# A softplus of which one VectorE operation becomes a sum of two products in PSUM, in a fused Mamba and feed-forward kernel

## What is computed

```python
x, z = split(hidden @ in_proj_w.T)              # 512 channels each
u = silu(causal_conv4(x) + conv_b)
dt_lo, B, C = split(u @ x_proj_w.T)             # 64, 16, 16
delta = softplus(dt_lo @ dt_proj_w.T + dt_proj_b)
h[t] = exp(delta[t] * A) * h[t-1] + delta[t] * u[t] * B[t]   # 512 x 16 states
y = (sum_n h * C + u * D) * silu(z)
x1 = layernorm(hidden + y @ out_proj_w.T)
f = gelu(gelu((silu(x1 @ w1) * (x1 @ w2)) @ h1) @ h2) @ w3   # with a scale per column
out = layernorm(x1 + f)
```

## Time and profile before

| | us |
|---|---|
| median of 3 runs (3010.54 to 3012.91) | 3012.06 |
| the profiled execution | 3011.42 |
| its span, first to last instruction | 3009.6 |
| mean granted clock of TensorE | 0.953 |

### The profile page before, as it was taken

The page is one execution under the profiler, slowest core; times in us unless marked ns, Lnnn a source line. Parts: engine busy times, 40 slices in busy tenths (PEclk is TensorE's granted clock), DMA queues, the critical chain, the costliest instruction groups (busy, mean ns, idle before and its releaser), DMA issues. The chain is left out here.

```text
span 3009.6 us, 40984 instructions
## 1 busy us (share of the span) xinstructions
PE 2720.0 (90%) x11540; PEld 1619.3 (54%) x11540; DVE 2297.7 (76%) x2650; ACT 2033.7 (68%) x3600; POOL 1704.2 (57%) x839
## 2 busy tenths in 40 slices
PE   5798998998998998998998976999999999999997
PEld 2243443343443443443443432778888888888886
DVE  6999999999999999999999999144445444444452
ACT  3878877878878877877878877465544555555452
POOL 4899999999899989999999998100000000000000
PEclk8899999998999999999999987999999999999999
DMA  8565565565566565565565566632222222222210
GB/s 265 122 188 158 144 190 158 144 193 164 134 193 165 136 192 159 139 196 158 139 192 165 143 186 224 205 101 77 92 70 70 84 91 77 70 79 88 70 42 15
DMA packets 239646, 412.05 MB, mean 137 GB/s; under 512 B 23264, under 2 KB 63456, under 8 KB 239456
## 3 DMA queue, kind: packets, MB, share of 16 engines
q1 hardware_dynamic: 175680, 297.67, 36.6%
q10 hardware_dynamic: 63776, 112.22, 11.4%
HBM read 285.55 MB, written 124.26 MB: 136 GB/s over the span
## 5 line engine op out<-in xcount | busy, mean ns | idle before, releaser
L1284 DVE TENSOR_TENSOR_SCAN h<-bank,state,db 128x512 f32<-128x512 f32 x1024 | 1243.3, 1268 | 18.9 <-ACT bank L916 18.5
L1144 POOL TENSOR_TENSOR hc<-h,c_rows 128x1024 f32<-128x1024 f32 x512 | 1200.3, 2375 | 96.6 <-DVE h L1284 75.0
L916 ACT ACTIVATE bank<-d_bc,a_neg 128x512 f32<-128x512 f32 x1024 | 695.4, 685 | 251.8 <-DVE h L1284 240.6
L1625 ACT ACTIVATE hring<-s_bank,sc 128x512 f32<-128x512 f32 x248 | 170.4, 687 | 488.6 <-PE s_bank L1558 488.3
L1558 PE MATMUL s_bank<-mid,h_r 128*128 128x512 f32 x2048 | 468.7, 390 | 4.6 <-DVEq L1652 4.6
L1268 DVE TENSOR_TENSOR db<-bank,du_bc 128x2048 f32<-128x2048 f32 x192 | 435.7, 2269 | 2.5 <-issue 2.5
L1558 PEld LDWEIGHTS s_bank<-mid,h_r 128*128 128x128 f32 x2048 | 385.5, 188 | 85.6 <-ACTq L1596 5.0
L731 PE MATMUL bank<-x_t,w 128*128 128x512 f32 x1088 | 362.5, 461 | 60.7 <-ACT ab L993 53.9
L659 PE MATMUL bank<-hc,fold_w 128*32 128x512 f32 x2048 | 305.1, 671 | 23.0 <-DVE uz L1308 11.3
L731 PEld LDWEIGHTS bank<-x_t,w 128*128 128x128 f32 x1088 | 203.2, 200 | 216.6 <-ACT ab L993 101.0
L1155 POOL TENSOR_TENSOR db<-du_bc,b_row 128x2048 f32<-128x2048 f32 x64 | 291.4, 4553 | 16.0 <-DVE h L1284 15.9
(11 more groups left out here) (147 smaller groups left out, 3721.7 us busy)
## 6 DMA issues: line engine op xcount, KB each, us to landing
ab<-ab ACTq DMA_DIRECT2D x272, 256.0 KB, 3.8
du_bc<-du_rows SPq DMA_DIRECT2D x256, 256.0 KB, 4.7
d_bc<-d_rows SPq DMA_DIRECT2D x256, 256.0 KB, 7.7
s_abr<-ab SPq DMA_DIRECT2D x120, 512.0 KB, 3.7
w<-w ACTq DMA_DIRECT2D x136, 256.0 KB, 3.1
d_rows<-sp_r SPq DMA_DIRECT2D x64, 256.0 KB, 2.0
du_rows<-sp_w SPq DMA_DIRECT2D x64, 256.0 KB, 3.1
x<-res SPq DMA_DIRECT2D x17, 512.0 KB, 8.8
```

The source lines that it names most:

```text
L916: act.activation(decays[DECAY_BANK[g]][:], d_bc[c % 2][:, j, :], ACT.Exp, scale=a_neg[:, g:g + 1]).then_inc(decay, 1)
L1144: pool.tensor_tensor(hc[:, k % HCSTEPS, at:at + HG], h[:, H_SLOT[k], at:at + HG], c_rows[:, q, :].unsqueeze(1).broadcast_to([P, HG, NT]), ...
L1284: dve.tensor_tensor_scan(h[:, H_SLOT[k], j, :], decays[DECAY_BANK[g]][:], db[:, k % DBSTEPS, j, :], state[:, g:g + 1], ALU.mult, ALU.add). ...
L1625: act.activation(hring[c % RING][:], p_h[m % HBANKS][:], ACT.Gelu, scale=sc[:, 2 + layer, m:m + 1]).then_inc(gelu, 1)
```

## The change

The subtraction of slot +4 is taken from VectorE. ScalarE now writes the logarithm to SBUF (`sp_ln`) and then turns sp_w into 1 - sp_w, in place. TensorE gets a new step, `logarithm_less`, in slot +4 behind `front`: it waits for both and adds them in p_dt by two float32 products with the identity matrix. VectorE's one operation in slot +5 is sp_e = min(p_dt, 0) + sp_e, and GpSimd adds instead of subtracting. The semaphore counts follow. The 2 KB of `sp_ln` per partition take the place of one buffer of the w1/w2 ring, which goes from four to three; the next tile's first pieces are then loaded in the order 2, 0, 1.

```diff
-ABRING, W12RING = 3, 4
+ABRING, W12RING = 3, 3
+        sp_ln = sb("sp_ln", [P, NT])
+            def logarithm_less(t, c):
+                pe.wait_ge(sp_act, t.count(5 * KI, 5 * c + 5))
+                pe.matmul(p_dt[:], w_id[:].bitcast(F32), sp_ln[:], start=True, stop=False)
+                pe.matmul(p_dt[:], w_id[:].bitcast(F32), sp_w[c % 2][:], start=False, stop=True).then_inc(sp_mm, 1)
...
+                    for now, c in dt_places(t, i, 4):
+                        if exists(now):
+                            logarithm_less(now, c)
                     if exists(nxt.following()):
                         early(nxt.following(), i)
...
                 elif step == 3:
                     act.wait_ge(dt_sb, t.count(KI, c + 1))
-                    act.activation(x_ps[:], sp_e[:], ACT.Ln, bias=1.0).then_inc(sp_act, 1)
+                    act.activation(sp_ln[:], sp_e[:], ACT.Ln, bias=1.0).then_inc(sp_act, 1)
+                    act.wait_ge(sp_act, n + 3)
+                    act.activation(sp_w[k][:], sp_w[k][:], ACT.Identity, scale=-1.0, bias=1.0).then_inc(sp_act, 1)
...
                 elif e % 2 == 1 and exists(t):
-                    load_w12(t.following(), m - KH)
+                    load_w12(t.following(), e // 2 % W12RING)
...
-                    pool.tensor_tensor(sp_r[k][:], sp_r[k][:], sp_e[:], ALU.subtract).then_inc(delta, 1)
+                    pool.tensor_tensor(sp_r[k][:], sp_r[k][:], sp_e[:], ALU.add).then_inc(delta, 1)
...
-            def softplus(t, c, step):
-                k = c % 2
-                if step == 4:
-                    dve.wait_ge(sp_act, t.count(4 * KI, 4 * c + 4))
-                    dve.scalar_tensor_tensor(out=p_dt[:], in0=sp_w[k][:], scalar=-1.0, in1=p_dt[:],
-                                             op0=ALU.add, op1=ALU.subtract).then_inc(sp_dve, 1)
-                elif step == 5:
-                    dve.wait_ge(sp_dve, t.count(2 * KI, 2 * c + 1))
-                    dve.scalar_tensor_tensor(out=sp_e[:], in0=p_dt[:], scalar=0.0, in1=sp_e[:],
-                                             op0=ALU.max, op1=ALU.subtract).then_inc(sp_dve, 1)
+            def softplus(t, c):
+                dve.wait_ge(sp_mm, t.count(KI, c + 1))
+                dve.scalar_tensor_tensor(out=sp_e[:], in0=p_dt[:], scalar=0.0, in1=sp_e[:],
+                                         op0=ALU.min, op1=ALU.add).then_inc(sp_dve, 2)
```

More of the change, by code:

```diff
@@ L305, in mamba_stage @@
         halo, silu_u, silu_z = sem("halo"), sem("silu_u"), sem("silu_z")
-        sp_act = sem("sp_act")
+        sp_act, sp_mm = sem("sp_act"), sem("sp_mm")
         sp_dve = sem("sp_dve")
@@ L712, in ffn_product @@
                 if which == 0:
-                    pe.wait_ge(w12_in[m % W12RING], t.count(16 * KH // W12RING, 16 * (m // W12RING + 1)))
+                    pe.wait_ge(w12_in[m % W12RING], t.count(16 * len(range(m % W12RING, KH, W12RING)), 16 * (m // W12RING + 1)))
                 before = product_before(t, e)
@@ L868, in softplus @@
                 k, x_ps = c % 2, p_dt
-                n = t.count(4 * KI, 4 * c)
+                n = t.count(5 * KI, 5 * c)
                 if step == 1:
@@ L1364, in tile @@
                             times_b(now, g // JC)
[L1365 to L1368, removed]
+                    for now, c in dt_places(t, i, 5):
+                        if exists(now):
+                            softplus(now, c)
                     if i == XD_SLOTS.stop + 1 and exists(nxt):
```

## The result

| | before | after |
|---|---|---|
| median, us | 3012.48 (3010.54 to 3012.91) | 3083.81 (3081.24 to 3095.59) |
| the profiled execution | 3011.42 | 3086.21 |
| its span | 3009.6 | 3084.3 |
| mean granted clock | 0.953 | 0.966 |

A forecast was written before the change was run, and what follows sets the result against it. VectorE was taken to bound the first stage; fifteen steady tiles of 3.57 us (53.6), with the ends 56, were added to 3011.4 for 3067 us. The eight-in-ten range was 3036 to 3106 us.

The forecast's parts named there:

- Chunk 0: Slots 23 to 25: pair ready at 1052.40, VectorE arrives at 1052.44; no stall, gain 0.59 us, margin 0.04.
- rival B: TensorE's pair takes 0.99 us instead of 1.98, so 0.6 us a tile: 3021 us; chance 8%.
- D: Rival: time comes out level, with stalls of 0.2 us each in chunks 1 to 3; chance 3%.
- The ring: w1/w2 ring with three buffers: costs nothing in a tile; 0 to 1 us in the closing products.
- The steady tile: Pair late by 1.74, 1.24 and 1.18 us in chunks 1 to 3, less 0.59 in chunk 0: 3.57 us longer.
- the clock: Slow 1.2 GHz stretches falling on TensorE's pairs: 0.3 us a tile, bound 0 to 3, cancelled against L1302's give-back.
- L1302's give-back: VectorE's wait at old L1302 after chunk 3 shrinks: up to 0.4 us a tile back, cancelled against the clock.
- The ends: Opening and closing instances of the chunks, which differ from the steady tiles: together +2 us, bound 0 to 5.
- Whatever is taken from it is gained in full: VectorE, busy 97.8% in mid first stage, has no room, so work removed from it is gained in full.
- rival A: Faster: pair always ready for VectorE, so 38 us of work and 11 us of L1291's waits gained: 2962 us; chance 6%.
- ScalarE's Identity: One added operation per chunk, delaying ScalarE by 0.56 us; costed at nothing, bound 0 to 0.56 us per chunk.
- Rival C: TensorE's lateness feeds on through ScalarE's copies and decays, or slow stretches hit pairs: 1 to 3 us a tile, 3082 to 3112; chance 18%.

The follow-up runs named there:

- e1: Kernel before with a w1/w2 ring of three buffers instead of four, nothing else changed: 3012.7 us, ratio 0.9999.
- e8: As e5, but TensorE makes no pair of products except one in the opening; ScalarE's Identity stays: 3014.2 us, ratio 1.0009 to the kernel before.
- e12: Changed kernel without the pair; VectorE's operation reads the unchanged step-size product x in p_dt and waits for ScalarE alone: 3011.6 us, ratio 0.9996 to before.
- e9: As e8, with ScalarE's added Identity left out too: 3001.4 us, ratio 0.9959 to the kernel before.
- e5: Changed kernel; the pair is made, but VectorE doesn't wait for it and reads the next scan's decays in PSUM: 3027.9 us, ratio 1.0051 to before.
- e3: Changed kernel with one product of the pair, the logarithm's, instead of two: 3049.5 us, ratio 1.0130 to the kernel before.
- e2: Changed kernel with VectorE's remaining softplus operation one slot later, +6 instead of +5: 3064.6 us, ratio 1.0175 to the kernel before.
- e4: Changed kernel; the pair is made, but VectorE doesn't wait for it and reads the logarithm in SBUF: 3055.0 us, ratio 1.0147 to before.
- e7: Changed kernel; in chunks 1 to 3, 1 - w and its product come earlier, VectorE's operation in slot +6 ahead of times_b: 3038.0 us, ratio 1.0086 to before.

## Why the prediction was right, and where its sum was off

**The mechanism held.** TensorE's order makes VectorE wait in three of four chunks. By my own sums the wait is the lateness, plus the 0.59 of L1291, plus the wait that L1291 itself had in the sample tile. Chunk 1: 1.74 + 0.59 + 0.20 = 2.53, measured 2.60. Chunk 2: 1.24 + 0.59 + 0.33 = 2.16, measured 2.27. Chunk 3: 1.18 + 0.59 + 0.80 = 2.57; measured 2.37 in two tiles, but 1.76 in the others, where L1291 had not waited. Chunk 0: no wait in any steady tile, in spite of a margin of 0.04, which was luck. The text itself said "1.7 to 2.3 us each", which forgot L1291's own waits and is too low for chunk 1. The pair takes 1.99 from its start to VectorE (forecast 2.02), 2.09 in chunk 1 behind a smaller product. That settles rival B (0.99), and with it D. The other signs held too: 49 waits for the pair in all (forecast about 45), and behind the sixtieth gate, the second stage included, only 3.3 us more.

**The ring** was put at nothing, and e1 shows no difference.

**The steady tile: 3.57 forecast, 4.45 measured.** Clean waits are 6.63 a tile (2.60 + 2.27 + 1.76); less four times 0.59, and less the 0.78 that L1291 used to wait (10.0 us in 12.8 tiles), 3.49 remain. So the stalls' term was right to 0.1. The rest is the clock, first of all: five waits of chunk 1, 4.29, 4.69, 3.73, 3.86 and 4.34, are 7.9 us above 2.60 together, 0.53 a tile where I took 0.3 and cancelled it against L1302's give-back. That give-back did not come: the waits at the former L1302, now L1309, are 7.3 us against 6.8. Both terms were bounded rightly and their balance was not nothing; they explain 0.5 of the 0.9. The last 0.4 has no single name in the trace.

The Trainium skill (TensorE: Matmul & The Clock Gate, on the clock gate) made me weigh a gain from a fuller TensorE. The mean clock did rise, from 0.953 to 0.966 by the two profiles, but slow stretches fell on the pair in 5 of 15 steady tiles, where VectorE waits for it. The mean agrees with the rule, and the mean didn't decide the time.

**The ends: 2 forecast, 7.9 measured** (4.6 and 3.3), bound 5. For its size this is the term most mis-sized, and it lies outside its bound. I had read the opening as a gain of 1.2. In the trace after, its chunk 1 waits 5.09, since its pair stands behind a spread that waits 10 us for times_b, and then runs at 1.2 GHz:

```profile
71.71 1.22 PE L639 MATMUL bank<-bc,w_spread 64*128 64x512 f32 x2 [10.05 <-DVE db L1281]
72.86 2.07 PE L623 MATMUL bank<-sp_ln,w_id 128*128 128x512 f32 x2
...
76.75 0.69 DVE L1302 SCALAR_TENSOR_TENSOR sp_e<-bank,sp_e 128x512 f32<-128x512 f32 x1 [5.09 <-PE bank L624]
```

With 15 tiles of 4.45 (66.8) the sum is 74.7. Against 56 the miss is 13 in the tiles and 6 at the ends; by the median it is 17 us, within the range.

**"Whatever is taken from it is gained in full" was false.** It is the step that failed, though it moved the forecast little. The 38 us can't be had, not even where no pair is made (e8, e12): VectorE, busy 97.8%, was level with the chain of decays and copies on ScalarE and of the products that these copies wait for. So rival A's 2962 was out of reach of a pair that is merely in time; its price was wrong, not only its chance. The page that I held beside it (the Trainium skill, Perfetto Trace Analysis, on relieving the most contended engine) would have sent the work the same way; e8 and e12, at 3014.2 and 3011.6 us, show no gain from it here.

**ScalarE's Identity was not free in itself.** I costed it at nothing, bound 0.56 a chunk, 36 us. It costs 13 us where no pair is made (e8 less e9). In the kernel after it can hide behind VectorE's stalls; no run takes it away there alone, so its share of the 71 us stays open.

**Was the sum right for the right reason?** Partly. Counted by runs from before: VectorE's operation taken away and the Identity added, about 0 (e12, e8) where I had -38 and 0; the pair on TensorE without anybody waiting on VectorE, +14 (e5 less e8) where I had nothing; VectorE's wait for it, +56 (after less e5). My chunk sums took VectorE's full lateness and gave back 0.59; they describe the kernel after, in which VectorE's stalls give ScalarE and TensorE time to catch up (its waits for decays stayed at 15.0). They held for the variant in which the stalls are shortened (e3, forecast 3036 to 3050, measured 3049.5) and failed for those in which they are gone (e2, e4, e5, e7, e8). In the kernel after VectorE's own time line adds up: 120.0 us of waits for the pair, less 38, less the 11.4 at L1291, are 71 of the 74.7 us. That the forecast met this case, and not one of the others, was partly luck, since it rested on a gain that no kernel here shows. Rival C, lateness that feeds on, is real in this sense: its time, 3082 to 3112, holds the measured one. Of its two mechanisms the first didn't appear in the kernel after (no new wait for decays), the second, slow stretches on the pairs, did, at 0.53 us a tile instead of its 1 to 3. What exactly fixes ScalarE's pace in e8 and e12 (its order, the products that it waits for, or the clock at which they run) is argued from waits alone, and it stays open.

## What to carry to other kernels

An operation moved from a full engine to one with room costs what the receiving queue's order makes it cost: write down for each place what stands ahead in that queue, and when the reader arrives. Before counting the relief of the fullest engine as a gain, look for the engine that runs level with it; an experiment that simply leaves the operation out tells it in one run. And look at each instance of the opening by itself: it has other neighbours than the steady tile.

## What the runs showed of the hardware

A VectorE operation with both inputs in SBUF (e4) took 1732 ns on average beside a working GpSimd, while the same form with one input in PSUM takes 691 (after) or 684 (e5):

```profile
L1303 DVE SCALAR_TENSOR_TENSOR sp_e<-sp_ln,sp_e x64: 666/2223/2793, 53.3 to 1856.2; 128x512 f32<-128x512 f32 x64
...
992.73 2.40 DVE L1303 SCALAR_TENSOR_TENSOR sp_e<-sp_ln,sp_e 128x512 f32<-128x512 f32 x1
```

Its least is 666 ns and its median 2223 (ns, least/median/most), about the length of one of GpSimd's products (L1157, 2403 ns on average there). Of the 64 operations 46 started while such a product ran, and all 46 ended 0.55 us (545 to 553 ns) after that product's end, whenever they had started; of the other 18, 17 took 666 to 682 ns. In e5 also 46 started while L1157 ran, and they took 664 to 693 ns. The Trainium skill (SBUF — State Buffer, on the shared port pair) says that such an operation contends with a GpSimd instruction that reads SBUF, and that the one that comes second is blocked until the other ends; these durations agree. Between e4 and e5 lie 27 us. For this kernel it means that while GpSimd multiplies by C, a sum whose inputs both lie in SBUF is dear on VectorE.

The two levels of TensorE's clock can be read off one pair of instructions: 1.02 us for L624 at 2.4 GHz, 1.91 at 1.2 GHz.
